# First attention: the three parts of the maxima are turned by a transposing DMA instead of TensorE and a copy on ACT

## The chip, the cores and the metric

The kernel runs on one core of a Trainium2 chip. The metric is the device time of one launch in microseconds (us). Before the change three runs gave 1146.13, 1148.74 and 1152.38 us; the median is 1148.74 us.

## The reference, cut to what matters

The model has four layers, each an attention over a context followed by a feed-forward part. Only the attention of the first layer is touched. `x` and `ctx` are four sequences of 256 tokens with 256 features; keys and values are shared by four heads.

```python
def _L0_xattn_ref(q, k, v, Wq, Wk, Wv, Wfc, bfc):      # q = layernorm(x), k = v = ctx
    EMBED, HEADS, GROUPS = 256, 32, 8
    GROUP_HEADS, HEAD_DIM = HEADS // GROUPS, EMBED // HEADS     # 4 and 8
    qh = (q @ Wq.T).reshape(N, S_, HEADS, HEAD_DIM).transpose(0, 2, 1, 3)
    kh = (k @ Wk.T).reshape(N, S_, GROUPS, HEAD_DIM).transpose(0, 2, 1, 3)
    vh = (v @ Wv.T).reshape(N, S_, GROUPS, HEAD_DIM).transpose(0, 2, 1, 3)
    kh = jnp.repeat(kh, GROUP_HEADS, axis=1)
    vh = jnp.repeat(vh, GROUP_HEADS, axis=1)
    score = jnp.einsum('bhqd,bhkd->bhqk', qh, kh) / math.sqrt(HEAD_DIM)
    attn = jax.nn.softmax(score, axis=-1)
    out = jnp.einsum('bhqk,bhkd->bhqd', attn, vh)
    return out.transpose(0, 2, 1, 3).reshape(N, S_, EMBED) @ Wfc.T + bfc
```

## The kernel before, in words

`attention_l0` works through eight groups `g` of four heads. The scores are computed twice. A first pass (`max_scores`, L525 to L535) has queries on the rows of PSUM, and VectorE takes the negated maximum of each query (`find_max`, L682). A second pass (L595) has keys on the rows, so the maximum of a query must be subtracted along the columns. That is done inside the matmul: the negated maxima, split into three bf16 parts, are written as three more rows (96 to 98) of the moving operand `Q`, against rows of ones in `K`. ACT then takes the exponential (L668), TensorE multiplies it with the values (`mix`, L551), ACT copies the sums out (`take_sum`, L650), and TensorE turns them back every four steps (`turn`, L561).

A step `s` is one group, one sequence and one half of its keys: 8 steps a group, 64 in all. Each of the first 54 steps also holds two units of the first pass, for scores that are 20 units ahead (`AHEAD`); a step is max, scores, max, mix. **A half group** `n = 2g + h` is 8 such units and four steps: 512 tokens of 4 heads. Its maxima travel from VectorE to `Q` in a chain that is written out by hand:

- POOL splits them into three bf16 parts (L630 to L633), which raises `split`;
- TensorE turns the parts (`turn_max`, L537 to L543, four 128x12 transposes on L541) into one of the three PSUM banks that it shares with the units of the first pass; it stands after step 4n-5, and those of halves 0 and 1 stand among the 20 first units;
- ACT copies the bank to `negmax_T` (`copy_max`, L637 to L643), after the exponential of step 4n-4; this raises `max_out`, and the unit that takes the same bank next waits for it (`wait_shared`);
- SP issues three DMAs (`load_max`, L481 to L486), one for each part, each of 4 pieces of 1 KB into one row of `Q`; the second pass of step 4n waits for them (`m_in`).

SP's queue holds everything in one fixed order: the loads of groups 1 to 3, then for every half `load_max(n)`, and behind each odd one from n = 3 on the loads of group g+3 (while there are any: six DMAs, L469 and L464; the first waits until the scores of group g-1 are done) and two or three weight loads for the next part of the layer (L513). ACT and VectorE have no DMAs here.

Of the kernel before, what the change touches and what calls it, by code (L numbers as in the profile page):

```python
# [16 lines left out]
BF16 = mybir.dt.bfloat16  # L17
# [3 lines left out]
ACT = mybir.ActivationFunctionType  # L21
# [3 lines left out]
P = 128  # L25
BATCH, SEQ, D = 4, 256, 256
TOK = BATCH * SEQ
NT = TOK // P
NC = D // P
HALF = TOK // 2  # L30
PARTS = 3
# [354 lines left out]
def attention_l0(core, Wq, Wk, Wv, VE, q8, k8, ones_dram, scale, prefetch):  # L386
# [11 lines left out]
    KD, GROUPS, PER, R8, RING, AHEAD = 64, 8, 4, 8, 4, 20  # L398
    PR = PARTS * R8
    RK, ROWS, LOW = 96, P, 64  # L400
    units = [("k", 0, KD, th) for th in range(2)] + [("q", c, P, th) for c in range(NC) for th in range(2)]
    NU = len(units)
    STEPS, MAXES = 2 * BATCH, PER * BATCH
# [5 lines left out]
    shared = []  # L409
    for m in range(AHEAD):  # L410
        shared.append(("max", m))
        if m in (AHEAD - 9, AHEAD - 1):
            shared.append(("turn_max", (m + 1 - (AHEAD - 8)) // 8))
    after_step = {}
    for s in range(NS):
        events = [("max", 2 * s + AHEAD), ("max", 2 * s + AHEAD + 1)] if 2 * s + AHEAD < NM_ALL else []
        tail_events = []
        if s % 4 == 3 and (s + 5) // 4 < HALVES:
            tail_events.append(("turn_max", (s + 5) // 4))
        if s % STEPS in (2, 6) and s >= STEPS:  # L420
            tail_events.append(("turn", 2 * (s // STEPS - 1) + (s % STEPS == 6)))
        after_step[s] = tail_events
        shared += events + tail_events
# [2 lines left out]
    shared_bank = lambda event: 5 + place_of[event] % 3  # L426

    names = ("projected", "v_projected", "high", "rest", "middle", "low", "stored_q0", "stored_q1",
             "padded", "cleared", "ones", "v_out", "k_ones", "prefetched", "max_scored", "maxed", "split", "max_turned", "max_out",
             "scored", "exped", "mixed", "summed", "turned", "inverted", "normed")  # L430
    (projected, v_projected, high, rest, middle, low, stored_q0, stored_q1,
     padded, cleared, ones, v_out, k_ones, prefetched, max_scored, maxed, split, max_turned, max_out,
     scored, exped, mixed, summed, turned, inverted, normed) = (core.sem(n) for n in names)
    q_in, k_in = ([core.sem(f"{n}{i}") for i in range(RING)] for n in ("q_in", "k_in"))
    stored_k = [core.sem(f"stored_k{i}") for i in range(PARTS)]
    m_in = [[core.sem(f"m_in{i}_{h}") for h in range(2)] for i in range(RING)]
    with ExitStack() as ctx:
        QP = core.sb(ctx, "q_parts", [P, NC, PARTS, TOK], BF16)
# [3 lines left out]
        K = core.sb(ctx, "K", [P, RING, TOK], BF16)  # L442
        NM = core.sb(ctx, "negmax", [P, GROUPS, NT, PER], F32)
        NR = core.sb(ctx, "negmax_rest", [P, 2, NT // 2, PER], F32)
        NP = core.sb(ctx, "negmax_parts", [P, 2, NT // 2, PARTS, PER], BF16)
        MT = core.sb(ctx, "negmax_T", [PARTS * PER, 2, HALF], BF16)
        E = core.sb(ctx, "E", [P, ERING, PER, SEQ], F32)
        OS = core.sb(ctx, "OS", [P, 2, TOK], F32)
        RD = core.sb(ctx, "RD", [P, 2, 4, PER], F32)
# [6 lines left out]
        with nc.Block() as block:  # L456
            @block.sync
            def _(sp):
# [20 lines left out]

                def load_max(n):  # L480
                    g, h = n // 2, n % 2  # L481
                    sp.wait_ge(max_out, n + 1)
                    for i in range(PARTS):
                        q = Q[RK + i:RK + i + 1, g % RING, :].rearrange("p (j t) -> p j t", t=TOK)
                        sp.dma_start(q[:, :, h * HALF:(h + 1) * HALF], MT[PER * i:PER * (i + 1), h, :]
                                     ).then_inc(m_in[g % RING][h], 16)  # L486

                for i, done in enumerate((high, middle, low)):
                    sp.wait_ge(done, 2)
# [16 lines left out]
                for n in range(HALVES):  # L506
                    load_max(n)
                    g = n // 2
# [8 lines left out]
            def _(pe):  # L517
                def wait_shared(event):
                    n = place_of[event]
                    if n >= 3:  # L520
                        kind, i = shared[n - 3]
                        pe.wait_ge({"max": maxed, "turn_max": max_out, "turn": normed}[kind], i + 1)

                def max_scores(m):
                    g, b, j = m // MAXES, m % MAXES // PER, m % PER  # L525
# [7 lines left out]
                                        Q[0:RK, g % RING, j * TOK + t * P:j * TOK + (t + 1) * P],  # L533
                                        K[0:RK, g % RING, b * SEQ:(b + 1) * SEQ], start=True, stop=True)
                    ins.then_inc(max_scored, 1)  # L535

                def turn_max(n):  # L537
                    pe.wait_ge(split, n + 1)
                    wait_shared(("turn_max", n))
                    for t in range(NT // 2):  # L540
                        ins = pe.transpose(core.bank_bf16(shared_bank(("turn_max", n)))[0:PARTS * PER, t * P:(t + 1) * P],  # L541
                                           NP[:, n % 2, t].rearrange("p i j -> p (i j)"), core.identb[:, :])
                    ins.then_inc(max_turned, 1)  # L543

                def mix(s):
                    g, b, kt = steps[s]
# [28 lines left out]
                ins.then_inc(v_projected, 1)  # L575
                pe.wait_ge(rest, NU)
                pe.wait_ge(v_out, 1)
                for kind, i in shared[:AHEAD + 2]:
                    if kind == "max":
                        max_scores(i)  # L580
                    else:
                        turn_max(i)
                for s, (g, b, kt) in enumerate(steps):
                    if 2 * s + AHEAD < NM_ALL:
                        max_scores(2 * s + AHEAD)
                    if s == 0:
                        pe.wait_ge(k_ones, 16)
                    if s % 4 == 0:
                        pe.wait_ge(m_in[g % RING][s % STEPS // 4], 16 * PARTS * (g // RING + 1))
                    if s >= 2:  # L590
                        pe.wait_ge(exped, s - 1)
                    keys = slice(b * SEQ + kt * P, b * SEQ + (kt + 1) * P)
                    q = Q[0:ROWS, g % RING, :].rearrange("p (j t) -> p j t", t=TOK)
                    for n in range(2):
                        ins = pe.matmul(core.bank(2 * (s % 2) + n).rearrange("p (j q) -> p j q", q=SEQ),  # L595
                                        K[0:ROWS, g % RING, keys], q[:, 2 * n:2 * n + 2, b * SEQ:(b + 1) * SEQ],
                                        start=True, stop=True)
                    ins.then_inc(scored, 1)
                    if 2 * s + AHEAD < NM_ALL:
                        max_scores(2 * s + AHEAD + 1)  # L600
                    if s >= MIX_LAG:
                        mix(s - MIX_LAG)
                    for kind, i in after_step[s]:
                        if kind == "turn_max":
                            turn_max(i)
                        else:
                            turn(i)
                for s in range(NS - MIX_LAG, NS):
                    mix(s)
                turn(HALVES - 2)  # L610
# [2 lines left out]
            @block.gpsimd  # L613
            def _(pool):
                pool.memset(K[LOW:P, :, :].bitcast(F32), 0.0).then_inc(padded, 1)
                for slot in range(RING):
                    pool.memset(Q[LOW:P, slot, :].bitcast(F32), 0.0).then_inc(padded, 1)
                pool.wait_ge(padded, 1 + RING)
                pool.memset(VE[:, :, :, :], 0.0).then_inc(cleared, 1)
                pool.wait_ge(cleared, 1)  # L620
                pool.memset(VE[:, :, :, 8], 1.0).then_inc(ones, 1)
                chain = Chain(pool, core.sem("pool_chain"))
                for n in range(HALVES):
                    g, h = n // 2, n % 2
                    pool.wait_ge(maxed, 8 * (n + 1))
                    if n >= 2:
                        pool.wait_ge(max_turned, n - 1)
                    whole = NM[:, g, 4 * h:4 * h + 4, :]
                    part_of = [NP[:, h, :, i, :] for i in range(PARTS)]
                    chain(pool.tensor_copy(part_of[0], whole))  # L630
                    chain(pool.tensor_tensor(NR[:, h], whole, part_of[0], ALU.subtract))
                    chain(pool.tensor_copy(part_of[1], NR[:, h]))
                    pool.tensor_tensor(part_of[2], NR[:, h], part_of[1], ALU.subtract).then_inc(split, 1)  # L633

            @block.scalar
            def _(act):
                def copy_max(n):  # L637
                    g, h = n // 2, n % 2
                    act.wait_ge(max_turned, n + 1)
                    if g >= 1:  # L640
                        act.wait_ge(m_in[(g - 1) % RING][h], 16 * PARTS * ((g - 1) // RING + 1))
                    act.activation(MT[:, h, :], core.bank_bf16(shared_bank(("turn_max", n)))[0:PARTS * PER, 0:HALF],  # L642
                                   ACT.Copy).then_inc(max_out, 1)  # L643

                def take_sum(s):
                    g, b, kt = steps[s]
                    if b == 0 and g >= 2:
# [5 lines left out]
                for n in range(NU + 1):  # L653
# [4 lines left out]
                    if n >= 1:  # L658
                        u, m = n - 1, units[n - 1][2]
                        act.wait_ge(rest, u + 1)  # L660
                        act.activation(part(u, 1), R[0:m, u, :], ACT.Copy).then_inc(middle, 1)
                copy_max(0)
                copy_max(1)
                for s in range(NS):
                    act.wait_ge(scored, s + 1)
                    if s >= ERING:
# [3 lines left out]
                                   ACT.Exp, scale=scale).then_inc(exped, 1)  # L670
                    if s > MIX_LAG and (s - MIX_LAG) % 2:
                        take_sum(s - MIX_LAG)
                    if s % 4 == 0 and 2 <= s // 4 + 1 < HALVES:
                        copy_max(s // 4 + 1)
                take_sum(NS - 1)

            @block.vector
# [1797 lines left out]
```

## Time and profile before

| | |
|---|---|
| median of three runs | 1148.74 us (1146.13 to 1152.38) |
| the profiled execution | 1146.27 us, its span 1144.3 us |
| TensorE, mean granted clock | 0.851 of full speed |
| TensorE matmul busy in the span | 931.5 us, 81% |
| VectorE, ACT, GpSimd busy | 54%, 47%, 22% |
| steps of the first attention | from 54.88 us to about 172 us of the span |

The span runs from the first instruction to the last of the one execution that was profiled. "Idle before" of a row is the time in which its engine did nothing just before it, with the instruction or DMA whose end released it. A row of SPq is an instruction that issues a DMA: its duration is the time that the issue takes on SP, not the transfer. A merged SPq row covers several issues and the waits between them. PEld is the weight load of a matmul, which overlaps the matmul before it.

### The profile page before, as it was taken

The numbers are of one execution on the slowest core, as the hardware profiler recorded it, in microseconds if no ns is written. First come the engines' busy times: TensorE is split into PE (matmuls) and PEld (weight loads), VectorE is DVE, ScalarE is ACT, GpSimd is POOL, SyncE is SP. The second block draws the span as 40 slices with busy tenths as digits, with TensorE's granted clock in tenths as the row PEclk, the third lists the DMA queues.
The fourth block names the chain that finished last, engine by engine and source line by source line (L and its number), as shares of the span: only waits on it lengthen the run. The fifth ranks groups of instructions, "written<-read, shape, count | busy, mean of one in ns | idle before, by whom it ended". The sixth has DMA issues, their size and how long they took to land. (4 is left out here: it accounts for less than half of the span.)

```text
span 1144.3 us, 15734 instructions
## 1 busy us (share of the span) xinstructions
PE 931.5 (81%) x5518; PEld 555.4 (49%) x5544; DVE 620.5 (54%) x1284; ACT 539.3 (47%) x807; POOL 254.8 (22%) x299
## 2 busy tenths in 40 slices
PE   5698887997895458899699547787776699999998
PEld 3244436665584144444367332343344556666665
DVE  4577745545145976354413938999996441111124
ACT  3166673222125745688431247998986122222211
POOL 4011000000000003144231104767675031000023
PEclk9599998998998689999899856555655799999999
DMA  3613301001480005765100936665653311111012
GB/s 124 146 34 77 84 12 42 0 1 51 103 63 28 0 17 177 185 139 81 47 1 1 349 129 120 129 108 112 107 100 70 111 46 60 43 46 46 28 46 84
DMA packets 116494, 90.07 MB, mean 79 GB/s; under 512 B 77829, under 2 KB 104655, under 8 KB 114639
## 3 DMA queue, kind: packets, MB, share of 16 engines
q1 hardware_dynamic: 111570, 81.87, 30.6%
q0 software_dynamic: 1536, 4.20, 1.2%
q10 hardware_dynamic: 3312, 3.02, 0.8%
q8 instruction: 45, 0.74, 0.3%
q14 instruction: 31, 0.25, 0.1%
HBM read 57.66 MB, written 16.38 MB: 65 GB/s over the span
## 5 line engine op out<-in xcount | busy, mean ns | idle before, releaser
L2268 ACT ACTIVATE sb_l_E<-PS,sb_l_NB,sb_L3SQS 128x1024 uint8<-128x1024 f32 x128 | 154.5, 1207 | 23.0 <-DVE sb_l_NB L2280 13.5
L2277 DVE TENSOR_REDUCE sb_l_NM<-PS 128x1 f32<-128x1024 f32 x128 | 155.4, 1214 | 3.8 <-PE PS L2247 3.8
L2247 PE MATMUL PS<-sb_l_K,sb_l_Q 128*128 128x512 bf16 x232 | 115.7, 590 | 43.0 <-ACT sb_l_E L2268 33.9
L2224 POOL CAST sb_l_ET<-sb_l_EP 128x1024 bf16<-128x1024 uint8 x128 | 129.4, 1043 | 64.1 <-DMA sb_l_EP<-sb_l_E 59.6
L682 DVE TENSOR_REDUCE sb_negmax<-PS 128x2 f32<-128x512 f32 x128 | 84.1, 689 | 32.2 <-PE PS L532 31.9
L1468 ACT ACTIVATE sb_hidden<-PS 128x512 f32<-128x512 f32 x39 | 23.3, 598 | 164.5 <-PE PS L1422 164.5
L1503 DVE TENSOR_TENSOR sb_hidden<-sb_hidden,PS 128x512 f32<-128x512 f32 x39 | 26.8, 687 | 125.1 <-ACT sb_hidden L1468 125.1
L2257 PEld LDWEIGHTS PS<-sb_L3VI,sb_l_ET 128*128 128x128 bf16 x1024 | 56.1, 113 | 69.1 <-issue 56.1
L668 ACT ACTIVATE sb_E<-PS 128x1024 f32<-128x1024 f32 x64 | 65.5, 1024 | 42.8 <-PE PS L595 42.8
L1422 PE MATMUL PS<-sb_L3w,sb_block_xT 128*128 x184 | 82.8, 592 | 0.0
L991 ACT ACTIVATE sb_E<-PS 128x1024 f32<-128x1024 f32 x64 | 65.3, 1024 | 24.7 <-PE PS L899 21.0
L532 PE MATMUL PS<-sb_K,sb_Q 96*128 96x256 bf16 x256 | 53.8, 302 | 15.8 <-ACT sb_negmax_T L642 10.3
L915 POOL MEMSET sb_rms_eps<- 128x1 f32 x1 | 0.1, 99 | 275.2 <-POOLq L175 275.2
L1422 PE MATMUL PS<-sb_W,sb_XT 128*128 128x512 f32 x128 | 59.1, 607 | 0.0
L2257 PE MATMUL PS<-sb_L3VI,sb_l_ET 128*128 128x16 bf16 x1024 | 50.8, 179 | 5.7 <-POOL sb_l_ET L2224 5.7
L1193 DVE SCALAR_TENSOR_TENSOR sb_X<-PS,sb_gates,sb_X 128x256 f32<-128x256 f32 x80 | 33.2, 476 | 35.7 <-PE PS L1116 35.7
L1422 PEld LDWEIGHTS PS<-sb_L3w,sb_block_xT 128*128 128x128 f32 x184 | 34.8, 190 | 34.4 <-issue 33.2
L200 PE MATMUL PS<-sb_identf,sb_XN 128*128 128x128 f32 x128 | 24.7, 374 | 32.3 <-DVE sb_XN L235 32.3
L532 PEld LDWEIGHTS PS<-sb_K,sb_Q 96*128 96x128 bf16 x256 | 21.3, 102 | 51.3 <-ACT sb_negmax_T L642 16.5
L595 PE MATMUL PS<-sb_Q,sb_K 128*128 128x512 bf16 x128 | 39.6, 391 | 5.3 <-DMA sb_Q<-sb_negmax_T 5.3
L1444 PE MATMUL PS<-sb_W2E,sb_hidden_T 128*128 x184 | 43.5, 379 | 0.0
L1375 POOL DMA_INDIRECT sb_XN<-ys,sb_slot x8 | 7.6, 952 | 160.0 <-PE PS L1444 157.8
(342 smaller groups left out, 1748.3 us busy)
## 6 DMA issues: line engine op xcount, KB each, us to landing
sb_Q<-q SPq DMA_DIRECT2D x48, 192.0 KB
sb_L3w<-L3w SPq DMA_DIRECT2D x16, 512.0 KB, 9.5
sb_K<-k SPq DMA_DIRECT2D x24, 192.0 KB
sb_W2E<-L3w SPq DMA_DIRECT2D x8, 512.0 KB, 9.4
q<-sb_q_parts SPq DMA_DIRECT2D x12, 256.0 KB, 2.4
xs<-zero_row SPq DMA_DIRECT2D x1, 2944.0 KB, 47.9
sb_block_x<-xs SPq DMA_DIRECT2D x23, 128.0 KB, 2.2
ys<-sb_block_y ACTq DMA_DIRECT2D x23, 128.0 KB, 2.4
```

The source lines that it names most:

```text
L532: ins = pe.matmul(core.PS[:, shared_bank(("max", m)), i * SEQ:(i + 1) * SEQ], Q[0:RK, g % RING, j * TOK + t * P:j * TOK + (t + 1) * P], K[ ...
L595: ins = pe.matmul(core.bank(2 * (s % 2) + n).rearrange("p (j q) -> p j q", q=SEQ), K[0:ROWS, g % RING, keys], q[:, 2 * n:2 * n + 2, b * SE ...
L668: act.activation(E[:, s % ERING].rearrange("p j q -> p (j q)"), core.PS[:, 2 * (s % 2):2 * (s % 2) + 2, :].rearrange("p b n -> p (b n)"), ...
L682: dve.tensor_reduce(NM[:, g, 2 * b:2 * b + 2, j:j + 1], core.bank(shared_bank(("max", m))).rearrange("p (u k) -> p u k", k=SEQ), axis=AX.X ...
L991: act.activation(E[:, s % ERING].rearrange("p j q -> p (j q)"), core.PS[:, 2 * (s % 2):2 * (s % 2) + 2, :].rearrange("p b n -> p (b n)"), ...
L1422: ins = pe.matmul(core.bank(2 * (u % 2) + side), x, w, start=(c == 0), stop=(c == NC - 1))
L1444: ins = pe.matmul(core.PS[:, 7, 0:D], HT[:, u % 2, k, :], w, start=(k == 0), stop=(k == HC - 1))
L2224: return eng.tensor_copy(ET[:, u % CRING], EP[:, u // 2 % TRING, :, :, u % 2])
L2247: ins = pe.matmul(core.bank(2 * (n % SRING) + half), Q[:, h % RING, t * P:(t + 1) * P], K[:, h % RING, half * HALF:(half + 1) * HALF], sta ...
L2257: ins = pe.matmul(core.PS[:, 6 + h % 2, t * HD:(t + 1) * HD], ET[:, u % CRING, k, :], VI[:, k, h * HD:(h + 1) * HD], start=(k == 0), stop= ...
L2268: act.activation(E[:, n // 2 % ERING, :, n % 2], S(n), ACT.Exp, bias=NB[:, n:n + 1], scale=scale_of(h, t), accum_out=ZS[:, n:n + 1]).then_ ...
L2277: dve.tensor_reduce(NM[:, n:n + 1], S(n), axis=AX.X, op=ALU.max, negate=True).then_inc(maxed, 1)
```

## The change

The parts now lie in one tile of 128 columns for each half of a group (12 rows for each head: part by part, four token tiles each), whose unused columns GpSimd zeroes once. `load_max` waits for `split`, issues a transposing DMA of this 128x128 bf16 tile (32 KB) into `negmax_T`, waits for it, and issues four DMAs, one for each head, that move 12 rows of 128 elements (256 bytes each) into the three rows of `Q`. `turn_max` on TensorE, `copy_max` on ACT and their place in the ring of shared banks are gone. POOL now waits for the transposing DMA of the half before last instead of TensorE's turn.

```diff
@@ attention_l0: the ring of shared banks
     for m in range(AHEAD):
         shared.append(("max", m))
-        if m in (AHEAD - 9, AHEAD - 1):
-            shared.append(("turn_max", (m + 1 - (AHEAD - 8)) // 8))
...
-        if s % 4 == 3 and (s + 5) // 4 < HALVES:
-            tail_events.append(("turn_max", (s + 5) // 4))
...
-        NP = core.sb(ctx, "negmax_parts", [P, 2, NT // 2, PARTS, PER], BF16)
-        MT = core.sb(ctx, "negmax_T", [PARTS * PER, 2, HALF], BF16)
+        NP = core.sb(ctx, "negmax_parts", [P, 2, P], BF16)
+        MT = core.sb(ctx, "negmax_T", [P, 2, P], BF16)
@@ SP
                 def load_max(n):
                     g, h = n // 2, n % 2
-                    sp.wait_ge(max_out, n + 1)
-                    for i in range(PARTS):
-                        q = Q[RK + i:RK + i + 1, g % RING, :].rearrange("p (j t) -> p j t", t=TOK)
-                        sp.dma_start(q[:, :, h * HALF:(h + 1) * HALF], MT[PER * i:PER * (i + 1), h, :]
-                                     ).then_inc(m_in[g % RING][h], 16)
+                    sp.wait_ge(split, n + 1)
+                    if g >= 1:
+                        sp.wait_ge(m_in[(g - 1) % RING][h], 16 * PER * ((g - 1) // RING + 1))
+                    sp.dma_start_transpose(MT[:, h:h + 1, :], NP[:, h, :]).then_inc(max_turned[h], 16)
+                    sp.wait_ge(max_turned[h], 16 * (g + 1))
+                    for j in range(PER):
+                        sp.dma_start(Q[RK:RK + PARTS, g % RING, j * TOK + h * HALF:j * TOK + (h + 1) * HALF],
+                                     MT[PARTS * 4 * j:PARTS * 4 * (j + 1), h, :]).then_inc(m_in[g % RING][h], 16)
@@ TensorE
-                def turn_max(n):
-                    pe.wait_ge(split, n + 1)
-                    wait_shared(("turn_max", n))
-                    for t in range(NT // 2):
-                        ins = pe.transpose(core.bank_bf16(shared_bank(("turn_max", n)))[0:PARTS * PER, t * P:(t + 1) * P],
-                                           NP[:, n % 2, t].rearrange("p i j -> p (i j)"), core.identb[:, :])
-                    ins.then_inc(max_turned, 1)
...
-                        pe.wait_ge(m_in[g % RING][s % STEPS // 4], 16 * PARTS * (g // RING + 1))
+                        pe.wait_ge(m_in[g % RING][s % STEPS // 4], 16 * PER * (g // RING + 1))
@@ POOL
+                chain(pool.memset(NP[:, :, :], 0.0))
                 for n in range(HALVES):
                     g, h = n // 2, n % 2
                     pool.wait_ge(maxed, 8 * (n + 1))
                     if n >= 2:
-                        pool.wait_ge(max_turned, n - 1)
+                        pool.wait_ge(max_turned[h], 16 * (n // 2))
                     whole = NM[:, g, 4 * h:4 * h + 4, :]
-                    part_of = [NP[:, h, :, i, :] for i in range(PARTS)]
+                    parts = NP[:, h, 0:PER * PARTS * 4].rearrange("p (j i t) -> p i t j", i=PARTS, t=4)
+                    part_of = [parts[:, i] for i in range(PARTS)]
@@ ACT
-                def copy_max(n):
-                    g, h = n // 2, n % 2
-                    act.wait_ge(max_turned, n + 1)
-                    if g >= 1:
-                        act.wait_ge(m_in[(g - 1) % RING][h], 16 * PARTS * ((g - 1) // RING + 1))
-                    act.activation(MT[:, h, :], core.bank_bf16(shared_bank(("turn_max", n)))[0:PARTS * PER, 0:HALF],
-                                   ACT.Copy).then_inc(max_out, 1)
...
-                    if s % 4 == 0 and 2 <= s // 4 + 1 < HALVES:
-                        copy_max(s // 4 + 1)
```

On SP, in the program before, this stands from the half n = 3 of the maxima over the loads of group 4 and three weight loads to the half n = 4 (`sb_negmax_T` are the turned maxima, `q` and `k` scratch in HBM):

```order
L485 DMA sb_Q<-sb_negmax_T 1x4x512 [waits max_out_54]
L485 DMA sb_Q<-sb_negmax_T 1x4x512 x2
L469 DMA sb_K<-k 24x1x1024 [waits scored_55]
L464 DMA sb_Q<-q 24x4096
...
L513 DMA sb_W2E<-L0gate 128x2x8
L513 DMA sb_L0w_31<-L0w 128x2x128
L513 DMA sb_L0b_34<-L0b 8x256
L485 DMA sb_Q<-sb_negmax_T 1x4x512 [waits max_out_54]
L485 DMA sb_Q<-sb_negmax_T 1x4x512 x2
```

And now, at the same place:

```order
L482 DMA_TRANSPOSE sb_negmax_T<-sb_negmax_parts 128x1x128 [waits m_in0_1_74,split_52]
L485 DMA sb_Q<-sb_negmax_T 3x4x128 [waits max_turned1_72]
L485 DMA sb_Q<-sb_negmax_T 3x4x128 x3
L466 DMA sb_K<-k 24x1x1024 [waits scored_53]
L461 DMA sb_Q<-q 24x4096
...
L513 DMA sb_W2E<-L0gate 128x2x8
L513 DMA sb_L0w_31<-L0w 128x2x128
L513 DMA sb_L0b_34<-L0b 8x256
L482 DMA_TRANSPOSE sb_negmax_T<-sb_negmax_parts 128x1x128 [waits m_in1_0_75,split_52]
L485 DMA sb_Q<-sb_negmax_T 3x4x128 [waits max_turned0_71]
L485 DMA sb_Q<-sb_negmax_T 3x4x128 x3
```

SP now issues five DMAs for a half instead of three, and stands still between the first and the second until the first has landed; the loads and the weights keep their places.

On TensorE, the end of one step and the beginning of the next, before (`sb_L0VE` are the values, `sb_negmax_parts` the parts of the maxima):

```order
L551 MATMUL PS<-sb_E,sb_L0VE 32x256 x4
L541 MATMUL PS<-sb_identb,sb_negmax_parts 12x128 x4
L532 MATMUL PS<-sb_K,sb_Q 128x256 x2
L595 MATMUL PS<-sb_Q,sb_K 128x512 x2
L532 MATMUL PS<-sb_K,sb_Q 128x256 x2
```

And now:

```order
L543 MATMUL PS<-sb_E,sb_L0VE 32x256 x4
L532 MATMUL PS<-sb_K,sb_Q 128x256 x2
L584 MATMUL PS<-sb_Q,sb_K 128x512 x2
L532 MATMUL PS<-sb_K,sb_Q 128x256 x2
```

Only the four small transposes are gone; nothing else changes its place on TensorE.

## Rows read from the trace of the kernel before

**Rows 1.** Waits, 62 to 158 us: total us, times, longest.

```profile
PEld PS L532 <- ACT sb_negmax_T L642: 16.5, 13, 1.3
```

**Rows 2.** Timeline, steps 5 to 12: start us, us, engine, line, operation.

```profile
64.62 0.39 PE L532 MATMUL PS<-sb_K,sb_Q 96*128 96x256 bf16 x2 [0.79 <-ACT sb_negmax_T L642]
...
67.30 0.22 POOL L633 TENSOR_TENSOR sb_negmax_parts<-sb_negmax_rest,sb_negmax_parts 128x16 bf16<-128x16 f32 x1
...
69.46 0.39 PE L532 MATMUL PS<-sb_K,sb_Q 96*128 96x256 bf16 x2
...
69.69 0.60 PE L595 MATMUL PS<-sb_Q,sb_K 128*128 128x512 bf16 x2
...
71.25 0.57 ACT L642 ACTIVATE sb_negmax_T<-PS 12x512 bf16<-12x512 bf16 x1
...
71.87 0.39 PE L532 MATMUL PS<-sb_K,sb_Q 96*128 96x256 bf16 x2 [0.79 <-ACT sb_negmax_T L642]
...
73.42 0.39 PE L532 MATMUL PS<-sb_K,sb_Q 96*128 96x256 bf16 x2
...
75.46 0.38 PE L532 MATMUL PS<-sb_K,sb_Q 96*128 96x256 bf16 x2
...
77.20 0.39 PE L532 MATMUL PS<-sb_K,sb_Q 96*128 96x256 bf16 x2
```

**Rows 3.** Timeline of SP's queue, 46 to 89 us.

```profile
46.03 27.62 SPq L485 DMA_DIRECT2D sb_Q<-sb_negmax_T  x12
73.69 0.67 SPq L469 DMA_DIRECT2D sb_K<-k  x1
...
77.30 0.42 SPq L513 DMA_DIRECT2D sb_W2E<-L0gate  x1
...
78.27 0.36 SPq L513 DMA_DIRECT2D sb_L0b<-L0b  x1
79.58 9.53 SPq L485 DMA_DIRECT2D sb_Q<-sb_negmax_T  x6
```

**Rows 4.** Line 485: issue time, ns min/median/max, first and last start.

```profile
L485 SPq DMA_DIRECT2D sb_Q<-sb_negmax_T x48: 572/573/642, 46.0 to 165.1; - x48
```

**Rows 5.** Windows: length, busy of PE, PEld, DVE, ACT, POOL; clock, DMA share, GB/s.

```profile
53.00:54.00 1.00, 0.00 (x0) 0.00 (x0) 0.00 (x0) 0.00 (x0) 0.00 (x0) 0.50 0.19 40
54.00:55.00 1.00, 0.12 (x1) 0.14 (x2) 0.00 (x0) 0.00 (x0) 0.00 (x0) 0.50 0.00 0
...
80.00:81.00 1.00, 1.00 (x12) 0.35 (x10) 0.96 (x2) 0.53 (x1) 0.00 (x0) 1.00 0.32 56
81.00:82.00 1.00, 1.00 (x11) 0.50 (x6) 0.80 (x2) 0.77 (x2) 0.42 (x2) 1.00 0.01 4
```

**Rows 6.** Timeline, first scores of the second pass (step 0).

```profile
54.88 1.01 PE L595 MATMUL PS<-sb_Q,sb_K 128*128 128x512 bf16 x2 [5.28 <-DMA sb_Q<-sb_negmax_T]
```

**Rows 7.** Line 2209, transposing DMAs of the fourth attention, 128x1024: issue time, landing.

```profile
L2209 SPq DMA_TRANSPOSE sb_l_EP<-sb_l_E x64: 1232/1233/1512, 694.4 to 874.3; - x64
DMA to landing us min/median/max: 3.0/3.1/4.9
```

**Rows 8.** Line 838, 128x2048, the second transposing DMA (quiet queue).

```profile
L838 SPq DMA_TRANSPOSE sb_k_parts<-sb_k_parts x1: 2029/2029/2029, 539.7 to 539.7; - x1
DMA to landing us min/median/max: 4.2/4.2/4.2
```

**Rows 9.** Line 838, the first one (issued behind six loads).

```profile
L838 SPq DMA_TRANSPOSE sb_k_parts<-sb_k_parts x1: 8177/8177/8177, 517.4 to 517.4; - x1
DMA to landing us min/median/max: 11.7/11.7/11.7
```

**Rows 10.** Windows of SP's view, behind those loads: length; clock, DMA share, GB/s.

```profile
520.00:521.00 1.00, 1.00 0.60 126
...
525.00:526.00 1.00, 1.00 0.66 117
```

**Rows 11.** DMA issues: a small load, KB and us to landing.

```profile
sb_L3router<-L3router SPq DMA_DIRECT2D x1, 8.0 KB, 1.7
```

More of the change, by code:

```diff
@@ L428, in attention_l0 @@
     names = ("projected", "v_projected", "high", "rest", "middle", "low", "stored_q0", "stored_q1",
-             "padded", "cleared", "ones", "v_out", "k_ones", "prefetched", "max_scored", "maxed", "split", "max_turned", "max_out",
+             "padded", "cleared", "ones", "v_out", "k_ones", "prefetched", "max_scored", "maxed", "split",
              "scored", "exped", "mixed", "summed", "turned", "inverted", "normed")
     (projected, v_projected, high, rest, middle, low, stored_q0, stored_q1,
-     padded, cleared, ones, v_out, k_ones, prefetched, max_scored, maxed, split, max_turned, max_out,
+     padded, cleared, ones, v_out, k_ones, prefetched, max_scored, maxed, split,
      scored, exped, mixed, summed, turned, inverted, normed) = (core.sem(n) for n in names)
@@ L435, in attention_l0 @@
     stored_k = [core.sem(f"stored_k{i}") for i in range(PARTS)]
+    max_turned = [core.sem(f"max_turned{h}") for h in range(2)]
     m_in = [[core.sem(f"m_in{i}_{h}") for h in range(2)] for i in range(RING)]
@@ L521, in wait_shared @@
                         kind, i = shared[n - 3]
-                        pe.wait_ge({"max": maxed, "turn_max": max_out, "turn": normed}[kind], i + 1)
+                        pe.wait_ge({"max": maxed, "turn": normed}[kind], i + 1)
                 def max_scores(m):
@@ L577, in _ @@
                 pe.wait_ge(v_out, 1)
[L578 to L582, printed above, removed]
+                for m in range(AHEAD):
+                    max_scores(m)
                 for s, (g, b, kt) in enumerate(steps):
@@ L603, in _ @@
                     for kind, i in after_step[s]:
[L604 to L607, printed above, removed]
+                        turn(i)
                 for s in range(NS - MIX_LAG, NS):
@@ L661, in _ @@
                         act.activation(part(u, 1), R[0:m, u, :], ACT.Copy).then_inc(middle, 1)
-                copy_max(0)
-                copy_max(1)
                 for s in range(NS):
```

## The prediction

> **What bounds the kernel now.** I read the waits of the first attention first, then its timeline step by step, then SP's queue, then the transposing DMAs that other parts of the kernel already hold.
>
> In the waits, one line stands out: 13 times TensorE's weight load for the first pass waits for ACT's copy of the turned maxima, up to 1.3 us each [rows 1]. The timeline shows why, and shows the rhythm of four steps. From the first-pass matmul (L532) that opens a step to the next: 69.46 to 71.87 is 2.41 us, with ACT's copy from 71.25 to 71.82 holding the shared bank; then 1.55, 2.04 and 1.74 us, together 7.74 us for a half group [rows 2]. The step of 1.55 us is the plain one: the reader is to see that TensorE goes without idle time there (no bracket on its row), with VectorE's two maxima and ACT's exponential inside it. The step of 2.04 us also holds the turn of the sums, the step of 1.74 us the turn of the maxima. The clock was granted in full in these steps (1.00 at 80 to 82 us) and at half, the 1.2 GHz level, around 54 us, where TensorE had stood idle [rows 5]. So this stage is bound by TensorE, plus one stall for each half group.
>
> The stage begins late: the first scores of the second pass start at 54.88 us, after 5.28 us of idle time, released by the DMA that brings the maxima [rows 6]. SP issued it at 46.03 [rows 3], behind the loads of the first groups, and the DMA engines were busy until the slice of 53 to 54 us (share 0.19, then 0.00) [rows 5].
>
> **What goes.** Each of the 13 stalls costs 2.41 - 1.55 = 0.86 us: 11.2 us. The turns of the maxima of halves 2 to 15 stand in the steps, 14 of them, 1.74 - 1.55 = 0.19 us each: 2.7 us [rows 1, 2]. Together 13.9 us. A half group then takes 7.74 - 0.86 - 0.19 = 6.69 us, a group 13.38 in place of 15.48. The two turns and copies before step 0 lie beside the loads that TensorE waits for anyway: nothing. POOL's work is the same, and its new memset lies before any maximum exists: nothing. The last copy, at the end of the stage, I leave out (0.57 us at most, the duration of one copy [rows 2]).
>
> **What the transposing DMA costs.** The first attention has none, so it is bounded. The fourth attention's moves 128x1024, eight tiles of 128x128: 1.233 us to issue, 3.0 us to landing at the least [rows 7]. The quiet one on L838 moves sixteen tiles: 2.029 and 4.2 us [rows 8]. A line through the two gives for one tile an issue of 1.233 - 7 x 0.0995 = 0.54 us, and a landing after 3.0 - 7 x 0.15 = 1.95 us. From below, a transfer of 8 KB lands after 1.7 us [rows 11]; from above, 3.0 us, as if seven tiles less saved nothing. I take 1.95. Cheaper than nothing it cannot be, as SP now waits for it. Each of the four DMAs behind it issues like those of L485, 0.573 us and 0.04 to the next [rows 4]: 2.45 us. The last begins 1.84 us after the first, and lands 1.7 us later.
>
> The Trainium skill speaks against this change: VectorE: "VectorE: DVE Perf Modes", section "The three transpose paths", puts a 128x128 bf16 transpose at 390 ns on TensorE and 1309 ns by the DMA crossbar, and its rules for kernel authors say to use TensorE where PSUM will do as the destination. The row agrees on the order (a turn adds 0.19 us to a step, the quickest transposing DMA took 3.0 us). If its 1309 ns were the whole wait, each wait would be 0.64 us shorter than mine, and the stage would run at TensorE's pace. By its rule of preference the kernel should get slower; the mechanism for that is the third rival.
>
> **At the start** the transposing DMA takes the place of the first L485 at 46.03 and stands behind the same loads, so I let it land at 54.5, just before the 54.88 of now. Then the four DMAs: 54.5 + 1.84 + 1.7 = 58.0. Nothing hides it: TensorE waits. Cost 58.0 - 54.88 = +3.1 us. Bounds: landing with the last load at 53.5 gives +2.1; a transposing DMA 1.3 us slower (3.0 in place of 1.7) gives +4.4.
>
> **In the steps** what matters is how long the way of a half is, and what SP's queue holds. The split of a half ends 67.30 + 0.22 - 64.62 = 2.90 us after the opening of step 4n-7 (this one is of half 3), and the scores that need it begin 0.23 us into step 4n [rows 2]. Seven steps at the new pace are 7 x 1.55 + 2 x 0.49 (two turns of sums) = 11.8 us, so the way has 11.8 + 0.2 - 2.9 = 9.1 us. It needs 0.1 + 1.95 + 1.84 + 1.7 = 5.6 us. So each half alone is in time.
>
> But the wait stands in SP's queue, with everything queued behind it. A half holds SP for 0.1 + 1.95 + 2.45 = 4.5 us, where the three issues of now took 1.84. Behind each odd half up to half 9 come six loads, 73.69 to 77.30 = 3.61 us, and three weight loads, 77.30 to 78.63 and 0.04 more = 1.37 us [rows 3]. And the transposing DMA behind them must let them drain: the DMA engines are still busy in 80 to 81 us (share 0.32) and free after 81 [rows 5], where a DMA issued at 78.67 alone would have landed at 80.6; I put down 0.5 us. One round of SP: 9.0 + 3.61 + 1.37 + 0.5 = 14.5 us. That is more than TensorE's 13.38 and less than the 15.48 of now. **SP becomes the pace** while there are loads.
>
> Walking it: step 8 comes at 69.69 + 3.1 - 0.5 - 0.86 = 71.4 (two turns at the half clock and one stall gone), step 16 needs half 4 at 84.8. SP: half 3 is split at 69.5, turned at 71.5, its DMAs issued by 74.0; loads to 77.6, weights to 79.0; half 4 turned at 81.5, its last DMA landed at 85.0. So step 16 is about 0.1 late. Steps 24 and 32 then come at SP's pace, 14.5 - 13.38 = 1.1 us late each, and step 40 only 0.7, as two weight loads stand there in place of three. From half 11 on no loads are left, a round is 9.0 + 1.0 = 10 us, and TensorE sets the pace again. Sum of these stalls: 2.9 us.
>
> **The sum:** -13.9 + 3.1 + 2.9 = -7.9 us. Against the profiled execution 1146.27 - 7.9 = 1138.4; that execution lies 2.5 us under the median of the runs, so on the median 1148.74 - 7.9 = 1140.9. I predict 1141 us. With a wait of 1.7 us for 1.95 the start is 0.25 cheaper and each round of SP 0.5: -9.7 us.
>
> **Rivals.**
>
> *The wait is half again as long and eats the gain (no change).* With 3.0 us for 1.95 (the quickest of the 64 rows [rows 7]) the start costs 4.2; halves 1 to 3 still have slack, half 4 comes 1.3 late; a round is 14.5 + 2.1 = 16.6 us, slower than now, so steps 24, 32 and 40 are 3.2, 3.2 and 2.8 late. -13.9 + 4.2 + 10.5 = +0.8 us: 1149.5. For it: no row shows one below 3.0. Against it: the sixteen-tile row needs 1.2 us more than the eight-tile one, so size does count.
>
> *The pace is kept by TensorE.* If a wait is 1.3 to 1.5 us or the loads don't hold it up, no step is late: -13.9 + 2.1 to 3.1 = about -11.3 us: 1137.4. Against it: the sum of SP's own issues and two waits.
>
> *The transposing DMA gets stuck behind the loads (slower).* The first L838 was issued right behind six loads and landed after 11.7 us, with an issue of 8.18 [rows 9]; the quiet one took 4.2 [rows 8]. That is 7.5 us for the same cargo. Here four of them, halves 4, 6, 8 and 10, stand behind six loads, and nothing of their delay is covered any more: with 7.5 for 0.5 us it is 4 x 7.0 = 28, so -7.9 + 28 = +20 us: 1169. It decides from a delay of 0.5 + 7.9 / 4 = 2.5 us on. Against it: there the DMA share was still 0.60 and 0.66 in the slices 3 and 8 us after the issue [rows 10], here it is 0.01 within 3 us of it [rows 5], since the loads of `K` are smaller (24x1024 against 24x4096). Half of such a delay would give +6 us. This is also where the skill's preference would come out.
>
> *That it doesn't do what it says* I give nothing: the order shows the transposing DMA in each place, and no turn on TensorE.
>
> **Chances.** A difference under 0.5% (5.7 us) is about what a measurement of this kernel cannot tell from no change. Forecast (SP's pace, -4 to -10 us) 0.46, of which 0.08 falls within 5.7 us; TensorE's pace 0.10; no change 0.27, which reaches from -5 to +5 us; stuck behind loads 0.17. So faster 0.38 + 0.10 = 0.48, same 0.08 + 0.27 = 0.35, slower 0.17. The likeliest case alone spans 1139 to 1145. For 8 in 10 I need the second rival whole, the first whole and the beginning of the third: 1136 to 1157.
>
> **What would show it.** Right: a first second-pass matmul at 57 to 59 us; plain steps of 1.55 us with no wait for ACT; the transposing DMA's issue near 0.54 us and its landing near 2 us; TensorE waiting for `Q<-negmax_T` at steps 24, 32 and 40, 1 us each, and not at odd halves; the stage 8 us shorter. Wrong: landings of 3 us and more in quiet stretches (first rival), steps 16 to 40 that begin 3 us late or more (third), none late (second). A longer issue of the four DMAs, of 12 pieces each for 4 now, would count 8 times a round: 0.1 us each is 3 us in the sum, and a plain step that doesn't come to 1.55 us would show a bound that I took for TensorE and was not.

## The result, and the profile after

The changed kernel takes 1155.86 us (median of 20 runs), the kernel before 1148.88 us beside it: ratio 1.0062, interval 1.0047 to 1.0077. It is slower by 7 us, where 8 us less were forecast. In the profiled executions (1156.07 and 1146.27 us) the last second-pass scores of the first attention start at 182.87 us in place of 172.02: the stage ends 10.9 us later and the span is 10.0 us longer, so the difference lies in and before this stage (behind it the two executions take 971.4 and 972.3 us). The medians differ by 7.0 us only: the profiled execution of the kernel before lies 2.6 us under its median.

The waits of the changed kernel between 40 and 190 us. L584 is the second pass (L595 before). Against [rows 1], ACT's copy is gone, and the DMA of the maxima has taken its place:

```profile
PE PS L584 <- DMA sb_Q<-sb_negmax_T: 23.9, 5, 10.3
PEld PS L584 <- DMA sb_Q<-sb_negmax_T: 14.7, 4, 5.9
```

The timeline shows where, at steps 0, 12, 16, 20, 24 and 40:

```profile
59.59 1.01 PE L584 MATMUL PS<-sb_Q,sb_K 128*128 128x512 bf16 x2 [10.33 <-DMA sb_Q<-sb_negmax_T]
...
79.14 0.60 PE L584 MATMUL PS<-sb_Q,sb_K 128*128 128x512 bf16 x2
...
89.43 0.60 PE L584 MATMUL PS<-sb_Q,sb_K 128*128 128x512 bf16 x2 [3.45 <-DMA sb_Q<-sb_negmax_T]
...
97.65 0.60 PE L584 MATMUL PS<-sb_Q,sb_K 128*128 128x512 bf16 x2
...
106.69 0.61 PE L584 MATMUL PS<-sb_Q,sb_K 128*128 128x512 bf16 x2 [2.21 <-DMA sb_Q<-sb_negmax_T]
...
144.71 0.61 PE L584 MATMUL PS<-sb_Q,sb_K 128*128 128x512 bf16 x1 [5.64 <-DMA sb_Q<-sb_negmax_T]
```

Step 0 comes 4.7 us later than in [rows 6]. Starts of every fourth step, read from the same rows of both traces:

| us between steps | before | after |
|---|---|---|
| 0 to 4, 4 to 8 | 7.56, 7.25 | 6.70, 6.18 |
| 8 to 12 | 7.74 | 6.67 |
| 12 to 16, 16 to 20 | 7.73, 7.73 | 10.29, 8.22 |
| 20 to 24, 24 to 28 | 7.74, 7.73 | 9.04, 8.21 |
| 28 to 32, 32 to 36 | 7.73, 7.73 | 9.09, 8.25 |
| 36 to 40, 40 to 44 | 7.83, 7.75 | 12.47, 8.54 |
| 44 to 48, 48 to 52 | 7.73, 7.73 | 6.67, 6.67 |

Where nothing is late, a half group takes 6.67 us: the stall and the turn are gone, as forecast. Where one is late, the half behind it takes 8.2 us or more with no wait in it. The windows show the clock that was granted there (columns as in [rows 5]), with no matmul at all in the 3 us before step 16:

```profile
86.00:89.00 3.00, 0.00 (x0) 0.00 (x0) 0.71 (x2) 0.20 (x1) 0.00 (x0) 1.00 0.02 4
89.00:92.00 3.00, 2.57 (x16) 1.05 (x17) 1.29 (x2) 1.02 (x1) 0.00 (x0) 0.79 0.08 17
92.00:95.00 3.00, 3.00 (x21) 1.14 (x23) 1.55 (x4) 1.70 (x3) 1.00 (x4) 0.64 0.02 4
```

Means of 0.79 and 0.64 are a mix of the full level and the half one, 2.4 and 1.2 GHz.

SP's queue from half 4 to half 6, where [rows 3] had three quick issues a half. A gap between a transposing DMA (L482) and the copies (L485), the four DMAs that move the turned rows into `Q`, is SP's wait:

```profile
81.55 1.14 SPq L482 DMA_TRANSPOSE sb_negmax_T<-sb_negmax_parts  x1
85.22 3.09 SPq L485 DMA_DIRECT2D sb_Q<-sb_negmax_T  x4
88.42 1.11 SPq L482 DMA_TRANSPOSE sb_negmax_T<-sb_negmax_parts  x1
90.70 2.96 SPq L485 DMA_DIRECT2D sb_Q<-sb_negmax_T  x4
93.70 0.70 SPq L466 DMA_DIRECT2D sb_K<-k  x1
...
98.08 0.92 SPq L513 DMA_DIRECT2D sb_L0w<-L0w  x2
99.05 0.32 SPq L513 DMA_DIRECT2D sb_L0b<-L0sb  x1
99.48 1.13 SPq L482 DMA_TRANSPOSE sb_negmax_T<-sb_negmax_parts  x1
102.51 3.08 SPq L485 DMA_DIRECT2D sb_Q<-sb_negmax_T  x4
```

SP is never without work between 81.55 and 102.51: each row begins where the one before, or its landing, ends. One round, 85.22 to 102.51, is 17.3 us. The next ends at 119.78, again 17.3. The third ends at 140.52, 20.7 us, and here its transposing DMA stands behind a weight load of 1 MB (`L0w`, 128x8x256):

```profile
131.92 0.92 SPq L513 DMA_DIRECT2D sb_L0w<-L0w  x2
132.95 1.34 SPq L482 DMA_TRANSPOSE sb_negmax_T<-sb_negmax_parts  x1
140.52 3.07 SPq L485 DMA_DIRECT2D sb_Q<-sb_negmax_T  x4
```

From step 16 to 24, 32 and 40 it is the same rhythm: 17.26, 17.30 and 20.72 us. The two new operations by themselves, over all 16 halves:

```profile
L482 SPq DMA_TRANSPOSE sb_negmax_T<-sb_negmax_parts x16: 1102/1114/1807, 45.5 to 171.0; - x16
DMA to landing us min/median/max: 2.3/2.3/9.8
```

```profile
L485 SPq DMA_DIRECT2D sb_Q<-sb_negmax_T x64: 697/699/848, 55.3 to 175.5; - x64
```

### The profile page after: what moved, and what is told of

Same layout as the page of the kernel before. It is cut to its first block and busy times, and to the rows that moved or that the text cites. A ratio compares the mean times of both kernels' runs of the same rounds, so it can differ in the third digit from the quotient of the medians.

```text
span 1154.3 us, 15608 instructions
## 1 busy us (share of the span) xinstructions
PE 934.6 (81%) x5454; PEld 552.8 (48%) x5480; DVE 620.2 (54%) x1284; ACT 531.8 (46%) x791; POOL 257.4 (22%) x300
## 5 line engine op out<-in xcount | busy, mean ns | idle before, releaser
L584 PE MATMUL PS<-sb_Q,sb_K 128*128 128x512 bf16 x128 | 41.7, 410 | 23.9 <-DMA sb_Q<-sb_negmax_T 23.9
L532 PE MATMUL PS<-sb_K,sb_Q 96*128 96x256 bf16 x256 | 56.3, 311 | 5.9 <-DMA sb_Q<-q 5.8
L543 PE MATMUL PS<-sb_E,sb_L0VE 128*32 128x256 f32 x512 | 42.9, 409 | 2.6 <-ACT sb_OS L630 2.6
```

The lines of the kernel that those rows point to most:

```text
L532: ins = pe.matmul(core.PS[:, shared_bank(("max", m)), i * SEQ:(i + 1) * SEQ], Q[0:RK, g % RING, j * TOK + t * P:j * TOK + (t + 1) * P], K[ ...
L543: ins = pe.matmul(core.PS[32 * j:32 * j + 32, 4, 0:SEQ], VE[:, 2 * b + kt, g, :], E[:, s % ERING, j, :], start=(kt == 0), stop=(kt == 1))
```

## The experiments

Three theories stood after the result. **SP's queue:** the sum of what SP issues and waits for in a round is the pace. **The DMA engines:** the transposing DMA is slow among loads, wherever it is issued. **The clock:** the half clock behind each wait is a cost of its own. The kernels ran on two other chips, the first four on one and the last four on the other, each beside the kernel before; times are compared through ratios, steps through each kernel's own trace. Two kinds of scatter limit what a single trace says. The changed kernel and the four experiments that are like it up to step 0 (weights_behind, keep_busy, loads_on_pool and weights_late) began that step at 57.79 to 61.24 us, so a stage is best counted from step 0. And behind the last scores every kernel runs the same program, but took 979 to 985 us there on the one chip and 982 to 988 on the other.

**weights_behind**

```diff
-                    if n % 2 and g >= 1:
-                        if g + RING - 1 < GROUPS:
-                            load(g + RING - 1)
-                        for dst, src in prefetch[g - 1::GROUPS - 1]:
+                    if n % 2 and g >= 1 and g + RING - 1 < GROUPS:
+                        load(g + RING - 1)
+                    if n % 2 == 0 and g >= 2:
+                        for dst, src in prefetch[g - 2::GROUPS - 1]:
                             sp.dma_start(dst, src).then_inc(prefetched, 16)
+                for dst, src in prefetch[GROUPS - 2::GROUPS - 1]:
+                    sp.dma_start(dst, src).then_inc(prefetched, 16)
```

> The changed kernel with the weight loads (L513) moved behind the even half of the maxima that follows them; the loads of Q and K stay. Theory (SP's queue sets the pace, and one transposing DMA waits behind a weight load of 1 MB): the transposing DMAs of halves 4, 6 and 8 are issued 1.4 us earlier, so step 16 is 2.2 us late in place of 3.6; the rounds of SP stay 17.3 us since nothing is taken out of them; half 10 no longer waits 7.6 us for its transposing DMA but about 3, so step 40 is 2 us late in place of 5.8, though half 11 now stands behind the 1 MB and may be 1 to 2 us late. Sum about -4 us against the changed kernel (1151 to 1153). Rival (the transposing DMA behind loads is slow by itself, whatever they are): step 40 as late as now, no change.

Ratio to before 1.008 (1.0050 to 1.0109); this can't be told from the changed kernel's 1.0062. Half of the expectation came: 36 to 40 took 10.19 us in place of 12.47, 12 to 16 took 8.42 in place of 10.29. But the rest of the rounds grew, steps 16 to 24 from 17.3 to 18.9 us, and from step 0 to the last scores the stage is 1.2 us longer, where 4 us less were expected. SP's queue shows why: now both halves stand behind something. The even one waits 4.1 us behind the loads, the odd one, which had waited 2.3, waits 3.3 behind the weights:

```profile
98.98 1.13 SPq L482 DMA_TRANSPOSE sb_negmax_T<-sb_negmax_parts  x1
103.06 3.07 SPq L485 DMA_DIRECT2D sb_Q<-sb_negmax_T  x4
106.17 0.93 SPq L513 DMA_DIRECT2D sb_L0w<-L0w  x2
107.14 0.32 SPq L513 DMA_DIRECT2D sb_L0b<-L0sb  x1
107.58 1.13 SPq L482 DMA_TRANSPOSE sb_negmax_T<-sb_negmax_parts  x1
110.88 2.99 SPq L485 DMA_DIRECT2D sb_Q<-sb_negmax_T  x4
```

So what is issued in front of a transposing DMA has a part: in both places its landing takes longer than the 2.3 us of a quiet queue, and a move that splits the loads into two places pays twice. That the rounds would keep their length was wrong.

**keep_busy**

```diff
+                    if s in (16, 24, 32, 40):
+                        pe.wait_ge(exped, s - 1)
+                        for i in range(26 if s == 40 else 13):
+                            pe.matmul(core.bank(2 * (s % 2)), core.identb[:, :], K[:, g % RING, 0:HALF], start=True, stop=True)
                     if s % 4 == 0:
                         pe.wait_ge(m_in[g % RING][s % STEPS // 4], 16 * PER * (g // RING + 1))
```

> The changed kernel with 13 matmuls of 512 columns (26 at step 40) into a bank that the step overwrites, in front of TensorE's wait for the maxima at steps 16, 24, 32 and 40: about 2.8 us of work at the full clock, 5.5 us at step 40. Theory (SP's round is the pace): the clock stays full and the half groups behind the waits take 6.7 us in place of 8.2 to 8.5, but that time comes back as a longer wait at the next late step, as SP's rounds stay 17.3 us; only the last one, after step 40, is gained: -2 us against the changed kernel. Rival (the half clock after each wait is a cost of its own): -1.55 us at each of four places and -0.3 more at the last, -6.5 us.

The clock stays full, and every half behind a late step takes 6.67 or 6.68 us. But steps 16 to 40 take 54.4 us in place of 55.3: the time came back in the waits. Step 0 to the last scores is 3.8 us shorter than in the changed kernel (119.5 in place of 123.3), 1.9 of them in steps 40 to 48. The clock is thus a real cost and mostly hidden behind SP. The whole launch doesn't confirm a gain (1.0097, 1.0065 to 1.0129), so this rests on one trace of each kernel. The window of the first steps behind the wait:

```profile
89.00:92.00 3.00, 3.00 (x26) 1.31 (x28) 1.37 (x3) 1.27 (x2) 0.00 (x0) 1.00 0.05 11
```

**loads_on_pool**

```diff
@@ SP, behind load_max(n)
-                    if n % 2 and g >= 1:
-                        if g + RING - 1 < GROUPS:
-                            load(g + RING - 1)
-                        for dst, src in prefetch[g - 1::GROUPS - 1]:
-                            sp.dma_start(dst, src).then_inc(prefetched, 16)
@@ GpSimd, behind the split (TensorE's wait for these loads, now late_in, is left out here)
                     pool.tensor_tensor(part_of[2], NR[:, h], part_of[1], ALU.subtract).then_inc(split, 1)
+                    if n % 2 == 0 and g >= 2:
+                        if g + RING - 2 < GROUPS:
+                            x = g + RING - 2
+                            pool.wait_ge(scored, STEPS * (g - 1))
+                            for r in range(PARTS):
+                                pool.dma_start(K[PR * r:PR * (r + 1), x % RING, :], ...).then_inc(late_in[x % RING], 16)
+                                pool.dma_start(Q[PR * r:PR * (r + 1), x % RING, :], ...).then_inc(late_in[x % RING], 16)
+                        for dst, src in prefetch[g - 2::GROUPS - 1]:
+                            pool.dma_start(dst, src).then_inc(prefetched, 16)
```

> The changed kernel with the loads of groups 4 to 7 and the weight loads issued by GpSimd, behind the split of the even half that follows; SP keeps only the transposing DMAs and the four copies of each half. Theory (what is queued on SP behind its wait sets the pace): a round of SP is 2 x 5.3 = 10.6 us, under TensorE's 13.4, so no step from 16 to 40 is late, every half group takes 6.7 us and the clock stays full: -20 us against the changed kernel, 1135 us, faster than the kernel before. Rival (the DMA engines, not SP's queue, are what the transposing DMAs wait for): they carry the same bytes, so the waits of 3 to 7.6 us and the late steps stay: 1150 us or more.

From step 8 to 52 half groups take 6.66 to 6.68 us, but for 12 to 16 (7.24) and 36 to 40 (9.14). The last scores start at 163.12 us, 19.8 us earlier than in the changed kernel. 1.8 of them lie before step 0, where the edit does nothing; the stage from step 0 on is 18.0 us shorter, near the 20 of SP's theory, with the same bytes in the DMA engines. The launch has a ratio of 0.9938 (0.9906 to 0.9971), 3 to 11 us less than the kernel before, which agrees with last scores 8.9 us earlier than there. The waits of TensorE:

```profile
PE PS L584 <- DMA sb_Q<-sb_negmax_T: 13.2, 3, 10.5
```

The rival was half right, and this is what parts the two theories. Among loads that another queue issues the transposing DMA is no quicker: those of halves 4, 6, 8 and 10 hold SP for 4.1 to 4.8 us, longer than the 3.0 to 3.7 of the changed kernel (here half 6, line 484 for 482 and 487 for 485):

```profile
88.77 1.12 SPq L484 DMA_TRANSPOSE sb_negmax_T<-sb_negmax_parts  x1
93.24 2.96 SPq L487 DMA_DIRECT2D sb_Q<-sb_negmax_T  x4
```

But no loads stand in that queue, and steps 24 and 32 are not late. At step 40 it is the copies that are slow: the first was issued at 119.58, beside the 1 MB load that GpSimd had just issued, and the step began 7.2 us later, where 4.2 us pass in a quiet round.

**copies_on_pool**

```diff
                     sp.dma_start_transpose(MT[:, h:h + 1, :], NP[:, h, :]).then_inc(max_turned[h], 16)
-                    sp.wait_ge(max_turned[h], 16 * (g + 1))
-                    for j in range(PER):
-                        sp.dma_start(Q[RK:RK + PARTS, ...], MT[...]).then_inc(m_in[g % RING][h], 16)
@@ GpSimd, behind the split
+                    pool.wait_ge(max_turned[h], 16 * (g + 1))
+                    for j in range(PER):
+                        pool.dma_start(Q[RK:RK + PARTS, ...], MT[...]).then_inc(m_in[g % RING][h], 16)
```

> The changed kernel with the wait for the transposing DMA and the four copies of each half moved to GpSimd; SP only issues the transposing DMA and goes on with its loads. Theory (SP's queue): a round of SP is 2 x 1.1 + 4.0 + 1.4 = 8 us, so SP is no longer the pace. GpSimd then holds a half for 1.2 us of split, 2.3 to 3.7 us of wait and four issues of about 1 us: 7.5 to 9 us against TensorE's 6.7, so it becomes the pace in turn: half groups of 7.5 to 9 us nearly everywhere, 1150 to 1165 us. Should its issues take 0.5 us or less, 1140 us. Rival (DMA engines): steps 16 to 40 late as now, the others not.

Ratio 0.9907 (0.9878 to 0.9936). The last scores start at 166.31 us; from step 0 on the stage is 16.3 us shorter than in the changed kernel. The expected 1150 to 1165 us were wrong: GpSimd did better than I had put down, as its four issues take 2.2 us, not 4:

```profile
88.12 2.19 POOL L620 DMA_DIRECT2D sb_Q<-sb_negmax_T  x4 [2.56 <-DMA sb_negmax_T<-sb_negmax_parts]
```

From step 8 on seven halves are up to 1 us longer than 6.67. The transposing DMA itself is the same as in the changed kernel (2.3 us to landing in the median); what changed is the queue that waits for it and issues the copies. The last scores are 5.7 us earlier than in the kernel before, the ratio is worth 7 to 14: part of the launch's gain is not in this trace of the stage.

**weights_late**

```diff
-                        for dst, src in prefetch[g - 1::GROUPS - 1]:
+                    if n >= 11:
+                        late = [p for i, p in enumerate(prefetch) if i != 10]
+                        for dst, src in (late[4 * (n - 11):4 * (n - 10)] if n < 15 else [prefetch[10]] + late[16:]):
                             sp.dma_start(dst, src).then_inc(prefetched, 16)
```

> The changed kernel with the weight loads (L513) taken out of the rounds up to half 10 and issued behind halves 11 to 15, four at a time, the one of 1 MB last. Theory (the sum of what SP issues and waits for in a round is the pace): the rounds that end at steps 24, 32 and 40 come to 15.9 us each in place of 17.3, 17.3 and 20.7; step 16 is 1.5 us earlier; step 44 comes 9 us earlier than in the changed kernel, counted from step 0, and the launch is about 9 us shorter unless the late weights hold up the end of the stage (up to +4). Rival (the loads of Q and K in the DMA engines alone set it): rounds of 17 us as now, and only step 40 comes earlier, by 3.5 us.

The rounds came to 15.8, 15.6 and 16.7 us for 15.9 expected. Step 44 comes 7.5 us earlier than in the changed kernel, counted from step 0. Ratio 0.9999 (0.9978 to 1.0021): 1.4 us of issues less in each round, and the 1 MB elsewhere, give back what the change had cost. Some of it may also be the weights' bytes, which no longer stand in front of a transposing DMA; the run doesn't part the two.

**early_after**

```diff
                 load(1)
-                load(2)
-                load(3)
                 sp.wait_ge(stored_q1, 16 * PARTS)
                 for n in range(HALVES):
                     load_max(n)
                     g = n // 2
+                    if n < 2:
+                        load(n + 2)
```

> The changed kernel with the loads of groups 2 and 3 behind the first and second half of the maxima instead of ahead of both. The first transposing DMA then has the loads of one group ahead of it, not of three: step 0 at 50.5 us in place of 59.6, -9 us. Theory (SP's round is the pace): the loads now stand in rounds that had none, so halves 1 and 2 become late instead (steps 4 and 8, about 3.5 us each and the half clock behind them), and from step 16 on all is as in the changed kernel, 1.5 to 3 us earlier: about -2 us of the 9. Rival (the late steps come from contention in the DMA engines): the 9 us are kept to the end.

Step 0 starts at 50.13 us, 9.5 us earlier, and steps 4 and 8 give it back:

```profile
50.13 1.01 PE L584 MATMUL PS<-sb_Q,sb_K 128*128 128x512 bf16 x2 [1.54 <-DMA sb_Q<-sb_negmax_T]
...
60.68 0.60 PE L584 MATMUL PS<-sb_Q,sb_K 128*128 128x512 bf16 x2 [2.80 <-DMA sb_Q<-sb_negmax_T]
...
70.92 1.03 PE L584 MATMUL PS<-sb_Q,sb_K 128*128 128x512 bf16 x2 [3.88 <-DMA sb_Q<-sb_negmax_T]
```

The last scores come 1.5 us earlier of the 9.5; ratio 1.0065 (1.0035 to 1.0095), as the changed kernel. An earlier start was worth little to a stage that SP's queue paces.

**early_before**, the same edit in the kernel before:

> The kernel before with the same move: the loads of groups 2 and 3 behind the first and second half. Its rounds of SP hold no wait for a landing (three issues a half, 1.84 us), so they have room for the loads: step 0 at 49.5 us in place of 54.9, and no new stall; -5 us against the kernel before, kept to the end. If the maxima's DMAs land late behind the loads, step 4 is up to 2 us late.

```profile
50.16 1.06 PE L595 MATMUL PS<-sb_Q,sb_K 128*128 128x512 bf16 x2
```

Step 0 starts 4.7 us earlier, without a wait for a DMA there or anywhere in the stage; the last scores start at 166.54 us, 5.5 earlier. Ratio 0.9947 (0.9930 to 0.9963). The same loads at the same place cost nothing where SP only issues.

**best**, both edits, the copies on GpSimd and the early start:

> The changed kernel with both: GpSimd waits for the transposing DMA and issues the four copies, and the loads of groups 2 and 3 stand behind the first and second half. SP's queue holds no wait for a landing any more, so the early start is kept: step 0 at 49.6 us (59.3 with the copies on GpSimd alone), later steps 0.3 to 0.8 us late at some halves as there. -16 us in the stage against the kernel before, -8 against the copies on GpSimd alone: ratio to the kernel before 0.984 to 0.988. Rival (contention): step 4 or 8 late by 3 us or more, and the gain of the early start gone.

Ratio 0.9851 (0.9827 to 0.9874), the fastest of all, faster than both kernels. Step 0 starts at 53.24, not at 49.6: the first copy was issued at 46.69 and the step began 6.6 us later, probably because the copies ran beside the loads of group 2 that SP had begun to issue at 45.27 (argued, not tried). The last scores start at 159.55 us, 12.5 us earlier than in the kernel before, of 16 expected. The ratio is worth 17 us (15 to 20), so some 5 us of the gain are not in this trace of the stage, and not explained. TensorE's waits:

```profile
PE PS L580 <- DMA sb_Q<-sb_negmax_T: 7.2, 5, 4.1
```

## Why the prediction was wrong

**What goes** was right. 13.9 us were forecast for the stalls and the turns; a half group without a late step takes 6.67 us for 6.69.

**The step that failed is the sum of one round of SP**, "9.0 + 3.61 + 1.37 + 0.5 = 14.5 us", which was to stay under the 15.48 us of before. It measured 17.3. The mechanism, SP as the pace while there are loads, was the one forecast, and four experiments that take work out of SP's queue or wait elsewhere bear it out (loads_on_pool, copies_on_pool, weights_late, best). Each term of the sum was low: the four copies take 3.0 to 3.2 us, not 2.45 (0.699 us each, where I had carried over the 0.573 of an issue with 4 pieces to one with 12, though the forecast named this as a thing that would count); the transposing DMA holds SP 2.28 us in a quiet queue, not 2.05, and 3.03 to 3.7 behind loads, not 2.55; the loads took 4.38 us in one round. Together: 3.20 + 2.28 + 3.00 + 4.38 + 1.40 + 3.03 = 17.3. In the next round the loads took 3.69 and the wait behind them 3.73, with the same sum. As a round lies above TensorE's 13.38, every tenth was paid three times over.

**Step 16**, put at 0.1 us late, was 3.6 late: the transposing DMA of half 4 was issued at 81.55 for 79.1 and landed at 85.22 for 81.5, and from the first copy to the step it took 4.2 us for 3.5. (The forecast sum of 2.9 left step 16 out altogether, which was 0.1 us then.)

**The 1 MB weight load** was not in the prediction at all. I read the weight loads of one round and took the others to be like it; the one ahead of half 10 made its wait 7.6 us and step 40 5.8 us late. The third rival, stuck behind loads, thus happened once in four: 5.3 us more than in a quiet queue, where the rival had 7.5 and needed 2.5 at each of the four places to decide the result.

**The half clock** was not in it either, though the rows showed the half level around the first idle time. It adds 1.5 us and more to each half behind a late step. keep_busy shows that most of it was covered by SP, and 1.9 us behind step 40 were not.

**The start** was put at +3.1 and measured +4.7, above the bound of 4.4. The transposing DMA landed at 55.3, not 54.5, and from the first copy's issue to step 0 it took 4.3 us, not 3.5. The 4.7 are of one pair of traces, and where the chain begins scatters; counted from the first issue of SP to step 0, the five kernels alike in this part took 14.0 to 14.7 us, the kernel before 8.9. So the start costs 5 us or more, whatever the single trace.

**The sum**, counted from the steps: -13.9 forecast for what goes; +4.7 start; steps 16, 24, 32, 40 late by 3.6, 2.4, 2.4 and 5.8 against 6.67, 14.2; the halves behind them 1.6, 1.5, 1.6 and 1.9, 6.6. That gives +11.6 against the 10.9 us of the trace (the medians moved by 7.0). Forecast were +3.1, +2.9 and nothing. The entries say where time appears and not what each would give back: without the 1.5 us behind steps 16, 24 and 32 the waits before the next late step grow, as keep_busy shows. The line through two sizes for the landing was not far off (1.95 for 2.3 us); that through the issues was (0.54 for 1.11 us, little under the 1.233 of eight tiles [rows 7]), and harmless, since the wait covers the issue. The first rival's 3.0 us gave a round of 16.6 us, near the 17.3 measured, for the wrong reason.

The page of the Trainium skill that spoke against the change, "VectorE: DVE Perf Modes", has in "The three transpose paths" 1309 ns for a 128x128 transpose by DMA. Here one landed 2.3 us after its issue at the least, and that is what a wait for it costs. The page's preference for TensorE, in "Rules for kernel authors", agrees with the result (1.0062), but with the wait in another queue the DMA path was the faster one (0.9907).

## What to carry to other kernels

A wait for a DMA inside a queue that issues other transfers counts in the sum of the whole queue's round, and it is this sum, not the wait's own length, that must stay under the pace: add up everything that the queue issues and waits for between two uses, every round by itself, the largest transfer too, before asking whether one item is in time. If the sum is near the pace of the bound engine, put the wait in a queue that has nothing behind it. And an earlier start or a faster engine gives little while that queue is the pace (1.5 us of 9.5 here).

## What the runs showed of the hardware

A transposing DMA of one 128x128 tile took nearly as long to issue as one of eight (1.11 and 1.233 us), and landed after 2.3 us, against 3.0 at the least. Behind loads of its own queue it took 3.0 to 3.7 us, behind one of 1 MB 7.6 us, and among loads that GpSimd issued 4.1 to 4.8 us. An issue of 12 short pieces took 0.699 us, of 4 pieces 0.573. The four copies took GpSimd 2.2 us to issue together, less than SP's 2.95. After waits of 2.2 to 5.6 us TensorE's clock fell to the half level (0.50 in the slices of 91 to 94 us, behind step 16), while the idle times of 0.8 us in the kernel before, twice a group, left it full (1.00 from 62 to 158 us).
